# An image tower on one core: the image rows for the second half of each patch are copied inside SBUF in place of a second load from main memory

## The chip, the cores and the metric

The kernel runs on one core of a Trainium2 chip. The core's engines run side by side, each its own program in order: PE (TensorE, matmuls into PSUM), ACT (ScalarE), DVE (VectorE), POOL (GpSimd) and SP (SyncE, which issues most DMAs). They wait for one another through semaphores. Sixteen DMA engines move the data between main memory and the on-chip memory SBUF. The metric is the device time of one execution in microseconds (us).

## What is computed

64 images of 3 x 224 x 224 are cut into patches of 16 x 16 pixels, 14 x 14 = 196 tokens an image. Two transformer layers with mixtures of experts follow:

```python
patches = img.reshape(B, C, Hp, p, Wp, p)
patches = patches.transpose(0, 2, 4, 1, 3, 5).reshape(B, S, C * p * p)
h = jnp.einsum('bsk,ek->bse', patches, w) + b                  # tok, 768 -> 128
h = h + L0_attn(_layernorm(h))     # single head, quantized weights, causal
h = h + L0_ffn(_layernorm(h))      # 8 experts, each takes its 1024 best tokens
h = h + L1_attn(_layernorm(h))     # 8 heads, layernorm on q and k, causal
h = h + L1_ffn(_layernorm(h))      # 8 experts, each token goes to its best 2
```

The change touches the first line of these only: how the pixels get into SBUF.

## The kernel before, in words

The program has four stages. The first, `embed_and_attend`, does patches, first attention and the routing logits of the first expert layer. It takes about the first 430 us. `topk_experts`, `attend_and_route` and `routed_experts` follow; they read what the first has written to main memory.

**Units and iterations.** The first stage works in 32 units of two images (4 tiles of 98 tokens, 392 columns). Its code is written out without a loop, and software-pipelined: iteration n works on the patches of unit n, the first layernorm of unit n-1, the scores of unit n-2, the output of unit n-3 and the second layernorm of unit n-4. ACT and POOL run one unit ahead with `pix`.

**Pixels.** `img` holds raw image rows, 96 partitions x 2 buffers x 2 images x 14 x 224 values. Partition 6r + c holds rows r of every patch of channel c as they are; partition 6r + 3 + c holds the same rows shifted left by 8 pixels. With this one column access at 16 k + j gives pixel j in the lower partitions and pixel j + 8 in the shifted ones, and a patch is embedded in 8 matmuls over 96 partitions. The copy from `img` to `pix` puts the columns j in order: ACT makes j = 0 to 3 (L568, two instructions), POOL j = 4 to 7 (L726, two). Both wait in `image_there` for the DMAs of that buffer (`img_loaded`) and until the unit two back is embedded. PE multiplies (L449, `patch`), ACT adds the bias and writes `hT` (L617).

**Order around the loads.** `load_images` issues twelve DMAs for a unit: for each of 2 images and 3 channels one for the plain rows (L300, 16 partitions x 14 x 224) and one for the shifted rows (L301, 16 x 14 x 216), both from main memory. Unit 0 is loaded in a first block, along with the weights (L305 to L309), while DVE and PE prepare the weights. That block ends for all engines at a barrier. In the second block `emit_sp` runs for n = 1 onwards: wait until the pixels of unit n-2 are copied (`pix_ready`, `pix_ready_pool`), load unit n; for n = 1 issue fourteen small early loads for later stages (L57); store normed tokens and h of unit n-7 (L422, L423), which waits for DVE (`h2_step`); store the logits of unit n-8 (L429), which waits for ACT (`lg_ready`). `img` has two buffers, so SP works about two iterations ahead of PE.

**ACT's order** matters at the start: in `emit_act` the pixels of unit n+1 stand before `hT` of unit n (see `emit` in the listing: `pixels(ahead, ...)`, then L617).

Of the kernel before, what the change touches and what calls it, by code (L numbers as in the profile page):

```python
# [11 lines left out]
IMAGES, CHANNELS, SIDE, PATCH = 64, 3, 224, 16  # L12
GRID = SIDE // PATCH
# [7 lines left out]
UNITS = IMAGES // 2  # L21
# [13 lines left out]
def wait(eng, sem, value, apart=False):  # L35

    if isinstance(value, int) and value <= 0:
        return
    eng.wait_ge(sem, value)
    if apart and not isinstance(value, int):  # L40


        eng.sem_inc(PASSED[str(eng.engine)], 1)  # L43
# [81 lines left out]
def straight(eng, emit, depth, count):  # L125

    for n in range(count + depth):
        emit(n, n)


def live(n, skew, count):
    return not isinstance(n, int) or 0 <= n - skew < count


def build(nc, x, L0_tok_w, L0_tok_b, L0_attn_Wq, L0_attn_Wk, L0_attn_Wv, L0_ffn_Wr, L0_ffn_W1, L0_ffn_b1,
# [3 lines left out]
    with ExitStack() as ctx:  # L139
# [38 lines left out]
        for i, g in enumerate(qk_gains):  # L178
# [3 lines left out]
        early.add(wr_all[:], L0_ffn_Wr)  # L182

        embed_and_attend(nc, sb, ps, sem, early, made, groups, x, L0_tok_w, L0_tok_b, L0_attn_Wq, L0_attn_Wk, L0_attn_Wv, L0_ffn_Wr,
                         hd_dram, ident, ident_b, ones, mask_qk, halfpow, logits_dram, xn_dram)
        chosen = topk_experts(nc, sb, ps, sem, early, wr_all, L0_ffn_W1, b1n_topk, L0_ffn_W2, L0_ffn_b2, hd_dram,
# [35 lines left out]
def span(start, size):  # L222

    return slice(start, start + size) if isinstance(start, int) else bass.ds(start, size)


def embed_and_attend(nc, sb, ps, sem, early, made, groups, x, w_tok, b_tok, wq, wk, wv, wr, hd_dram, ident, ident_b, ones,
                     mask_qk, halfpow, logits_dram, xn_dram):
    with ExitStack() as ph:
        S = lambda name, shape, dt=F32: sb(name, shape, dt, ph)  # L230
        P = lambda name, shape, dt=F32: ps(name, shape, dt, ph)
        half = PATCH // 2
        rows = CHANNELS * PATCH

        img = S("img", [2 * rows, 2, 2, GRID * SIDE])
# [52 lines left out]
        w_copied = sem("w_copied")  # L288
        cstep = sem("const_step")
        n_loads = 6  # L290
        img_loaded = [sem(f"img_loaded{k}") for k in range(2)]
        imgs = x.rearrange("b c (g p) w -> b c p g w", p=PATCH)

        def load_images(sp, u, k):

            for m in range(2):
                dst = img[:, k % 2, m, :].rearrange("r (g w) -> r g w", g=GRID)
                for c in range(CHANNELS):
                    lo, hi = (slice(CHANNELS * s + c, 2 * rows, 2 * CHANNELS) for s in range(2))
                    sp.dma_start(dst[lo], imgs[2 * u + m, c]).then_inc(img_loaded[k % 2], 16)  # L300
                    sp.dma_start(dst[hi, :, 0:SIDE - half], imgs[2 * u + m, c, :, :, half:]  # L301
                                 ).then_inc(img_loaded[k % 2], 16)

        def load_weights(sp):
            sp.dma_start(w_nat[:], w_tok).then_inc(w_loaded, 16)  # L305
            sp.dma_start(bias[:], b_tok.rearrange("(e o) -> e o", o=1)).then_inc(w_loaded, 16)
            for i, w in enumerate((wq, wk, wv)):
                sp.dma_start(w3[:, i, :], w).then_inc(w_loaded, 16)
            sp.dma_start(wr_sb[:], wr).then_inc(w_loaded, 16)  # L309

        with nc.Block() as block:
            @block.sync
            def _(sp):
                load_weights(sp)
                load_images(sp, 0, 0)

            @block.gpsimd
            def _(pool):
# [90 lines left out]
        def emit_sp(sp):  # L409
            def emit(n, k):  # L410

                if live(n, 0, UNITS) and not (isinstance(n, int) and n == 0):
                    wait(sp, pix_ready, 2 * (n - 1), apart=True)
                    wait(sp, pix_ready_pool, 2 * (n - 1))
                    load_images(sp, n, k)
                if isinstance(n, int) and n == 1:
                    early.issue(sp)
                if live(n, 7, UNITS):
                    u = n - 7
                    r = u % 2  # L420
                    wait(sp, h2_step, (u + 1) * H2_STEPS)
                    sp.dma_start(xn_view[:, span(u * TPU, TPU), :], xn2[:, r]).then_inc(xn2_stored[r], 16)  # L422
                    sp.dma_start(hd_view[:, span(u * TPU, TPU), :], h2[:, r]).then_inc(h2_stored[r], 16)  # L423
                if live(n, 8, UNITS):
                    u = n - 8
                    r = u % 2
                    wait(sp, lg_ready, u + 1)
                    for t in range(TPU):
                        sp.dma_start(logits_dram[:, span(u * COLS + t * TILE, TILE)],  # L429
                                     lg[32 * t:32 * t + EXPERTS, r, :]).then_inc(lg_stored[r], 16)  # L430
            straight(sp, emit, 8, UNITS)
            for s in (*xn2_stored, *h2_stored):
                sp.wait_ge(s, 16 * UNITS // 2)
            for s in lg_stored:
                sp.wait_ge(s, 16 * TPU * UNITS // 2)
# [119 lines left out]
            return img[:, k % 2].rearrange("r m (q j) -> r j (m q)", j=PATCH)[:, js, :]  # L555

        def image_there(eng, n, k):
            wait(eng, img_loaded[k % 2], (n // 2 + 1) * 16 * 12 if isinstance(n, int) else
                 (n - (k % 2)) * (16 * 6) + 16 * 12, apart=True)
            wait(eng, embedded, n - 1, apart=True)  # L560

        def emit_act(act):
            def pixels(n, k, first, end):
                if not live(n, 0, UNITS):
                    return
                if first == 0:
                    image_there(act, n, k)
                act.copy(pix[:, k % 2, first:end, :], by_column(k, slice(first, end))).then_inc(pix_ready, 1)  # L568
# [168 lines left out]
        with nc.Block() as block:  # L737
            @block.sync
            def _(sp):
                emit_sp(sp)  # L740

            @block.tensor
            def _(pe):
                emit_pe(pe)

            @block.scalar
            def _(act):
                emit_act(act)

            @block.vector  # L750
            def _(dve):
                emit_dve(dve)

            @block.gpsimd
            def _(pool):
                emit_pool(pool)
# [1750 lines left out]
```

## Time and profile before

| | us |
|---|---|
| median of 3 runs | 1961.18 |
| lowest and highest | 1959.18, 1964.82 |
| profiled execution, first to last instruction (span) | 1907.7 |
| what the median has beyond that span | 53.5 |

| engine | busy, share of the span |
|---|---|
| PE | 1666.0 us, 87% |
| DVE | 1201.1 us, 63% |
| POOL | 1162.9 us, 61% |
| ACT | 1076.6 us, 56% |
| DMA queue q1 (issued by SP) | 206432 packets, 134.16 MB, 28.9% of 16 engines |

The profile is of one execution. Busy shares are averages over four stages with different limits, so the first stage is read by itself, in windows of its time. PE's busy time includes waiting inside its pipeline. A time given with a DMA instruction of SP is how long its issue took; when the data had landed is a number of its own ("to landing"). The image loads are 192 of 196.0 KB and 192 of 189.0 KB, with a median of 4.3 and 4.5 us from issue to landing. The granted clock is a share of TensorE's full 2.4 GHz: 0.50 is the 1.2 GHz level.

### The profile page before, as it was taken

Reading aid. Unit: us, or ns where it says so; the run is one execution under the profiler, and the core shown is the slowest. Engines: PE = TensorE matmul, PEld = TensorE weight load, DVE = VectorE, ACT = ScalarE, POOL = GpSimd, SP = SyncE. Lnnn points to the kernel's source line nnn. Section 1 sums busy time; section 2 is a strip of 40 time slices with the busy share of each in tenths; the row PEclk is TensorE's granted clock in tenths of the full one; section 3 lists DMA queues with packets and bytes.
Section 4 is the critical chain, followed back from the end, with each engine's and each line's share of the span. In section 5 each row is a group of like instructions: output and inputs, shape, how many; then the busy total and the mean of one; then the engine's idle time right before and its main releaser. Section 6 shows DMA issues by size and latency. Waiting matters only on the chain. (4 is left out here: it accounts for less than half of the span.)

```text
span 1907.7 us, 45923 instructions
## 1 busy us (share of the span) xinstructions
PE 1666.0 (87%) x13765; PEld 1251.6 (66%) x13766; DVE 1201.1 (63%) x4836; ACT 1076.6 (56%) x2574; POOL 1162.9 (61%) x1108
## 2 busy tenths in 40 slices
PE   4999999995569764699999999999994999999996
PEld 2666666663447543467667677676662999998995
DVE  2899999983743002678888888888864343433442
ACT  2666666651436432467776776777751555555553
POOL 2455655531057885226776766767656687878876
PEclk8999999995569887699999999999997999999998
DMA  8989999931014433311111111211112455545553
GB/s 198 237 209 222 216 223 234 228 97 52 12 40 78 67 53 60 106 32 48 53 53 51 53 55 46 58 51 53 41 45 62 66 71 65 69 68 65 72 67 40
DMA packets 257801, 172.48 MB, mean 90 GB/s; under 512 B 25598, under 2 KB 250656, under 8 KB 257632
## 3 DMA queue, kind: packets, MB, share of 16 engines
q1 hardware_dynamic: 206432, 134.16, 28.9%
q0 software_dynamic: 50112, 35.64, 13.8%
q8 instruction: 92, 1.51, 0.3%
q10 hardware_dynamic: 1088, 0.53, 0.2%
q14 instruction: 77, 0.63, 0.1%
HBM read 117.64 MB, written 52.40 MB: 89 GB/s over the span
## 5 line engine op out<-in xcount | busy, mean ns | idle before, releaser
L2373 POOL DMA_INDIRECT out_dram<-r_yw,r_idx x212 | 332.5, 1568 | 94.2 <-issue 41.4
L2255 POOL DMA_INDIRECT rows_scratch<-routed_row,slot_u x256 | 254.2, 993 | 169.8 <-DVE slot_u L2194 106.7
L2438 ACT ACTIVATE r_hT<-r_p_up,r_b1T 128x256 f32<-128x256 f32 x424 | 191.6, 474 | 123.4 <-PE r_p_up L2413 120.0
L1920 ACT ACTIVATE a_probsT<-a_p_sc 98x392 f32<-98x392 f32 x384 | 170.7, 501 | 109.7 <-PE a_p_sc L1677 72.0
L2401 PEld LDWEIGHTS r_p_y<-w_all,r_hT 128*128 128x128 f32 x1696 | 224.1, 193 | 11.1
L2413 PE MATMUL r_p_up<-r_xgT,r_w1e 128*128 128x256 f32 x848 | 222.4, 386 | 9.3 <-DVE r_w1e L2453 8.7
L2401 PE MATMUL r_p_y<-w_all,r_hT 128*128 x1696 | 224.8, 276 | 0.0
L449 PE MATMUL p_embed<-pix,w_pix 96*128 96x392 f32 x512 | 209.2, 516 | 3.5 <-ACT pix L568 3.5
L2025 DVE TENSOR_REDUCE a_negmax<-a_p_max 98x2 bf16<-98x392 f32 x256 | 132.5, 559 | 61.4 <-PE a_p_max L1642 61.4
L718 POOL TENSOR_SCALAR vare<-mv 98x4 f32<-98x4 f32 x64 | 29.9, 467 | 218.3 <-DVE mv L703 199.5
L2413 PEld LDWEIGHTS r_p_up<-r_xgT,r_w1e 128*128 128x128 f32 x848 | 147.1, 194 | 22.5 <-issue 8.0
L2459 DVE TENSOR_TENSOR r_yb<-r_p_y,b_all 128x256 f32<-128x256 f32 x106 | 45.0, 425 | 133.5 <-PE r_p_y L2401 130.8
L1666 PE MATMUL a_p_sc<-q_var,kT 32*98 32x196 f32 x1024 | 117.2, 346 | 1.7 <-ACT a_probsT L1920 1.7
L896 POOL DMA_INDIRECT h_scratch<-yw,tok_u x64 | 100.4, 1568 | 28.0 <-issue 18.3
L726 POOL COPY pix<-img 96x784 f32<-96x784 f32 x64 | 95.8, 1526 | 31.6 <-DMA img<-in_x_dram 31.6
L449 PEld LDWEIGHTS p_embed<-pix,w_pix 96*128 96x128 f32 x512 | 89.5, 199 | 38.2 <-issue 6.3
L1703 PE MATMUL a_p_q<-wqkvT,a_xnT 128*98 128x384 f32 x256 | 107.9, 528 | 1.4 <-ACT q_var L1961 0.8
L568 ACT COPY pix<-img 96x784 f32<-96x784 f32 x64 | 98.3, 1542 | 19.1 <-DMA img<-in_x_dram 19.0
L886 POOL DMA_INDIRECT xg<-xn_scratch,tok_u x64 | 62.0, 969 | 75.1 <-DVE tok_u L1183 55.9
L2453 DVE COPY r_w1e<-w_all 128x512 f32 x106 | 48.4, 457 | 85.1 <-issue 60.5
L1201 DVE TENSOR_TENSOR yb<-p_y,b2e 128x512 f32<-128x512 f32 x16 | 11.1, 692 | 142.7 <-PE p_y L1014 142.7
L1014 PEld LDWEIGHTS p_y<-w2e,ffn_hT 128*128 128x128 f32 x512 | 69.8, 201 | 35.8 <-issue 34.4
(377 smaller groups left out, 4171.6 us busy)
## 6 DMA issues: line engine op xcount, KB each, us to landing
img<-in_x_dram SPq DMA_DIRECT2D x192, 196.0 KB, 4.3
img<-in_x_dram SPq DMA_DIRECT2D x192, 189.0 KB, 4.5
r_xg<-rows_scratch SPq DMA_DIRECT2D x106, 130.0 KB
xn_scratch<-xn SPq DMA_DIRECT2D x32, 196.0 KB
h_scratch<-h SPq DMA_DIRECT2D x32, 196.0 KB
h<-h_scratch SPq DMA_DIRECT2D x32, 196.0 KB
h3b<-h_scratch SPq DMA_DIRECT2D x32, 196.0 KB
out_dram<-h SPq DMA_DIRECT2D x32, 196.0 KB
```

What stands on the lines that cost most here:

```text
L449: last = pe.matmul(p_embed[:, 0:COLS], w_pix[:, j, :], pix[:, k % 2, j, :], start=(j == 0), stop=(j == half - 1))
L568: act.copy(pix[:, k % 2, first:end, :], by_column(k, slice(first, end))).then_inc(pix_ready, 1)
L896: pool.indirect_dma_start(hd_dram, bass.IndirectOffsetOnAxis(ap=tok_u[:, u * GT + t:u * GT + t + 1], axis=0), yw[:, u % RINGY, t, :], None ...
L1666: pe.matmul(p_sc[p][:, x * PAIR:(x + 1) * PAIR], kT[rows, s4, o:o + TILE], q_var[rows, s4, var + x, o:o + PAIR], start=(x == 0), stop=Fals ...
L1703: pe.matmul(p_q[t % 2][0:TILE, 0:3 * D], xnT[:, u % 2, t * TILE:(t + 1) * TILE], wqkvT[:], start=True, stop=True).then_inc(qkv, 1)
L1920: act.activation(probsT[:, u % 2, i, :], p_sc[i % 2][:, 0:2 * PAIR], ACT.Exp).then_inc(exped, 1)
L2025: dve.tensor_reduce(negmax[:, u % 2, group + 1, h], src.rearrange("p (h c) -> p h c", h=2), X, ALU.max, negate=True).then_inc(maxed, 1)
L2255: pool.indirect_dma_start(rows_dram, bass.IndirectOffsetOnAxis(ap=slot_u[:, u % ROWS, c, t:t + 1], axis=0), row[:, u % ROWS, c, t, :], Non ...
L2373: pool.indirect_dma_start(acc_dram, bass.IndirectOffsetOnAxis(ap=idx[:, (k - 3) % 4, t:t + 1], axis=0), yw[:, (k - 3) % 4, t, :], None, co ...
L2401: last = pe.matmul(p_y[k % 2][:, t, :], hT[:, (k - 2) % 2, f, t * 128:(t + 1) * 128], w2e[:, bass.ds(e, 1), f, :], start=(f == 0), stop=(f ...
L2413: pe.matmul(p_up[f][:, 0:G], w1e[:, (k - 1) % 2, f * 128:(f + 1) * 128], xgT[:, (k - 1) % 2, :], start=True, stop=True).then_inc(up, 1)
L2438: act.activation(hT[:, (k - 1) % 2, f, :], p_up[f][:, 0:G], ACT.Silu, bias=b1T[:, bass.ds(e * FC + f, 1)]).then_inc(act_h, 1)
```

## The change

The plain rows are loaded as before. The shifted rows are no longer loaded: `shift_images` waits until all six loads of the unit have landed and then issues six DMAs from SBUF to SBUF. Each takes the 16 partitions of one channel and image, from value 8 to the end of the 14 x 224 = 3136, and writes these 3128 values as one run to the partition three further on. (The values that cross a row's end land where no column is read.) The count that ACT and POOL wait for falls from 12 DMAs to 6, now the copies.

```diff
+        img_rows_in = sem("img_rows_in")
...
                 for c in range(CHANNELS):
+                    sp.dma_start(dst[c:2 * rows:2 * CHANNELS], imgs[2 * u + m, c]).then_inc(img_rows_in, 16)
+
+        def shift_images(sp, u, k):
+
+            sp.wait_ge(img_rows_in, (u + 1) * 16 * 2 * CHANNELS)
+            for m in range(2):
+                for c in range(CHANNELS):
                     lo, hi = (slice(CHANNELS * s + c, 2 * rows, 2 * CHANNELS) for s in range(2))
-                    sp.dma_start(dst[lo], imgs[2 * u + m, c]).then_inc(img_loaded[k % 2], 16)
-                    sp.dma_start(dst[hi, :, 0:SIDE - half], imgs[2 * u + m, c, :, :, half:]
+                    sp.dma_start(img[hi, k % 2, m, 0:GRID * SIDE - half], img[lo, k % 2, m, half:GRID * SIDE]
                                  ).then_inc(img_loaded[k % 2], 16)
...
                 load_images(sp, 0, 0)
+                shift_images(sp, 0, 0)
...
                                      lg[32 * t:32 * t + EXPERTS, r, :]).then_inc(lg_stored[r], 16)
+                if live(n, 0, UNITS) and not (isinstance(n, int) and n == 0):
+                    shift_images(sp, n, k)
...
-            wait(eng, img_loaded[k % 2], (n // 2 + 1) * 16 * 12 if isinstance(n, int) else
-                 (n - (k % 2)) * (16 * 6) + 16 * 12, apart=True)
+            wait(eng, img_loaded[k % 2], (n // 2 + 1) * 16 * 2 * CHANNELS, apart=True)
```

Only SP's row of instructions changes; it has 765 before and 507 after. At the start of the second block (L57: early loads, the first and the last shown) before:

```order
L300 DMA img<-in_x_dram 16x14x224
L301 DMA img<-in_x_dram 16x14x216
...
L57 DMA a_w_nat<-in_L_attn_Wq_dram 128x128
...
L57 DMA wr_all<-in_L_ffn_Wr_dram 128x8
L300 DMA img<-in_x_dram 16x14x224 [waits pix_ready_pool,pix_ready]
L301 DMA img<-in_x_dram 16x14x216
```

and after:

```order
L300 DMA img<-in_x_dram 16x14x224 x6
L57 DMA a_w_nat<-in_L_attn_Wq_dram 128x128
...
L57 DMA wr_all<-in_L_ffn_Wr_dram 128x8
L308 DMA img<-img 16x3128 [waits img_rows_in]
L308 DMA img<-img 16x3128 x5
L300 DMA img<-in_x_dram 16x14x224 [waits pix_ready_pool,pix_ready]
L300 DMA img<-in_x_dram 16x14x224 x5
```

The second half of unit 1's rows moved from before the early loads to behind them. In a full iteration on SP, before (twelve image loads, of which three are shown, then the stores):

```order
L300 DMA img<-in_x_dram 16x14x224 [waits pix_ready_pool,pix_ready]
L301 DMA img<-in_x_dram 16x14x216
L300 DMA img<-in_x_dram 16x14x224
...
L422 DMA xn_scratch<-xn 98x4x128 [waits h2_step]
L423 DMA h_scratch<-h 98x4x128
L429 DMA logits_scratch<-lg 8x98 [waits lg_ready]
L429 DMA logits_scratch<-lg 8x98 x3
```

and after:

```order
L300 DMA img<-in_x_dram 16x14x224 [waits pix_ready_pool,pix_ready]
L300 DMA img<-in_x_dram 16x14x224 x5
L430 DMA xn_scratch<-xn 98x4x128 [waits h2_step]
L431 DMA h_scratch<-h 98x4x128
L437 DMA logits_scratch<-lg 8x98 [waits lg_ready]
L437 DMA logits_scratch<-lg 8x98 x3
L308 DMA img<-img 16x3128 [waits img_rows_in]
L308 DMA img<-img 16x3128 x5
```

The stores moved ahead of the second half of the image, and a wait stands between.

## Rows read from the trace of the kernel before

**Rows 1.** The page's slices (40 of 47.7 us): busy tenths of the DMA engines.

```profile
DMA  8989999931014433311111111211112455545553
```

**Rows 2.** Windows: stretch, its length, busy us (instructions) by engine, PEclk, DMA share, GB/s.

```profile
84.80:97.20 12.40, 11.98 (x72) 7.91 (x71) 11.32 (x42) 8.20 (x19) 5.75 (x5) 1.00 1.03 245
...
399.40:411.80 12.40, 11.98 (x72) 7.88 (x71) 11.52 (x44) 8.40 (x20) 6.05 (x7) 1.00 0.13 35
```

**Rows 3.** Timeline, ACT: start, duration, instruction [idle before]; hT of units 18, 29, 30.

```profile
263.52 0.59 ACT L617 ACTIVATE hT<-p_embed,bias 128x392 f32<-128x392 f32 x1 [0.41 <-PE p_embed L449]
...
397.73 0.59 ACT L617 ACTIVATE hT<-p_embed,bias 128x392 f32<-128x392 f32 x1 [0.42 <-PE p_embed L449]
409.93 0.59 ACT L617 ACTIVATE hT<-p_embed,bias 128x392 f32<-128x392 f32 x1 [0.42 <-PE p_embed L449]
```

**Rows 4.** Waits, 0 to 60 us: who waited for whom, us in total, times, longest.

```profile
POOL pix L726 <- DMA img<-in_x_dram: 31.6, 4, 13.3
...
ACT pix L568 <- DMA img<-in_x_dram: 19.0, 2, 11.0
```

**Rows 5.** Timeline, SP: first load of a unit, first store, logits stores.

```profile
234.90 0.59 SPq L300 DMA_DIRECT2D img<-in_x_dram  x1
...
242.68 0.58 SPq L422 DMA_DIRECT2D xn_scratch<-xn  x1
...
243.80 1.92 SPq L429 DMA_DIRECT2D logits_scratch<-lg  x4
```

**Rows 6.** Image loads to landing (16 to 30 us, 100 to 390 us); window 75 to 400 us.

```profile
DMA to landing us min/median/max: 3.3/4.2/5.2
...
DMA to landing us min/median/max: 2.8/4.3/5.8
...
75.00:400.00 325.00, 306.68 (x1812) 203.24 (x1811) 304.17 (x1110) 212.31 (x493) 168.56 (x191) 0.99 0.94 221
```

**Rows 7.** Timeline, ACT: the first copy of the pixels of unit 19.

```profile
256.05 1.53 ACT L568 COPY pix<-img 96x784 f32<-96x784 f32 x1
```

**Rows 8.** DMA issues: transfer, number, KB each, median us to landing.

```profile
lgt<-logits_scratch SPq DMA_DIRECT2D x1, 392.0 KB, 3.0
...
block_rec<-rec SPq DMA_DIRECT2D x8, 24.9 KB, 2.1
```

**Rows 9.** Timeline, SP: first image load, first early load, first load of unit 2.

```profile
3.67 0.76 SPq L300 DMA_DIRECT2D img<-in_x_dram  x1
...
23.07 0.60 SPq L57 DMA_DIRECT2D a_w_nat<-in_L_attn_Wq_dram  x1
...
30.70 0.65 SPq L300 DMA_DIRECT2D img<-in_x_dram  x1
```

**Rows 10.** Timeline, ACT's copies of units 0, 1, 2, 4, and PE on units 1, 2.

```profile
16.60 2.93 ACT L568 COPY pix<-img 96x784 f32<-96x784 f32 x2
...
27.63 2.92 ACT L568 COPY pix<-img 96x784 f32<-96x784 f32 x2 [8.10 <-DMA img<-in_x_dram]
...
31.97 7.68 PE L449 MATMUL p_embed<-pix,w_pix 96*128 96x392 f32 x16
...
43.76 2.92 ACT L568 COPY pix<-img 96x784 f32<-96x784 f32 x2 [10.95 <-DMA img<-in_x_dram]
...
47.22 1.09 PE L455 MATMUL p_htr<-ident,hT 128*98 128x128 f32 x4 [7.56 <-ACT hT L617]
...
63.76 1.54 ACT L568 COPY pix<-img 96x784 f32<-96x784 f32 x1
```

**Rows 11.** A window as in rows 2, and PE's timeline (idle before in brackets).

```profile
122.00:124.00 2.00, 1.75 (x6) 1.40 (x7) 1.78 (x11) 1.65 (x7) 0.07 (x1) 0.50 1.09 264
...
122.25 1.09 PE L455 MATMUL p_htr<-ident,hT 128*98 128x128 f32 x4 [2.24 <-ACT hT L617]
...
123.14 2.82 PE L449 MATMUL p_embed<-pix,w_pix 96*128 96x392 f32 x4
...
239.45 1.48 PE L449 MATMUL p_embed<-pix,w_pix 96*128 96x392 f32 x4
```

## The prediction, made before the changed kernel ran
> **What bounds the kernel now.** I read the page's slices first [rows 1]: the image stage is the first nine or so of 40 (0 to 430 us), and there the DMA engines show 8 or 9 tenths throughout. PE is as full: 11.98 us of 12.40 in a window inside the stage [rows 2]. Two resources look full, and the change takes work from one of them only. So the question is which of the two paces the stage.
>
> Two views answer it. The first is the list of ACT's writes of hT, one for each unit of two images [rows 3]: from unit 18 (263.52 us) to unit 30 (409.93) they stand 146.41 / 12 = 12.20 us apart, without exception. The second is the pair of windows in [rows 2], one with the image traffic at its fullest (DMA share 1.03, 84.8 to 97.2 us), one after the last load (0.13, 399.4 to 411.8). PE is busy 11.98 us in both, ACT 8.20 and 8.40, DVE 11.32 and 11.52, and the hT of unit 30, made without image traffic, still comes 12.20 us after that of unit 29. When the traffic is gone, nothing speeds up. An iteration is paced by the ring of PE, DVE and ACT. **The DMA engines are full but not late.**
>
> The waits agree [rows 4]: all waiting for image data in the first 60 us is 31.6 us of POOL in four waits and 19.0 us of ACT in two, and the same view of 60 to 400 us has no wait for img on any engine.
>
> **The change in a full iteration.** Today SP needs 242.68 - 234.90 = 7.8 us for the twelve loads of a unit, 0.65 each, and 243.80 + 1.92 - 242.68 = 3.0 us for six stores [rows 5]: 10.8 of 12.2 us. After the change: six loads, 3.9 us. The same six stores, 3.0 us, which now come 3.9 us earlier. A wait until the six loads have landed. Then six copies inside the chip. The stores stand between the loads and the wait and cover most of it: the last load is issued 3.25 us into the unit and lands 4.3 us later (median of 100 to 390 us, [rows 6]), at 7.55 us, and the stores end at 6.9. That leaves 0.65 us of waiting.
>
> The issue of a copy isn't in the trace. From below stands a logits store, 1.92 / 4 = 0.48 us, from above an image load, 0.65 us [rows 5]. I take 0.48: the copy (16x3128) is a plain set of rows on both sides like that store, while the load is 16x14x224. Six cost 2.9 us. SP's unit becomes 3.9 + 3.0 + 0.65 + 2.9 = 10.4 us of 12.2, so it still idles for 1.8 us. Queued behind the new wait are the copies and then the next unit's loads and stores. Those loads may start only when the pixels of the unit two back are copied, and that happens once in 12.2 us in any case.
>
> The landing of a copy isn't in the trace either. The nearest rows are block_rec, a transfer within SBUF of 24.9 KB, 2.1 us, and for size lgt, 392 KB in rows of 3 KB, 3.0 us [rows 8]. Above them stands the short-run image load, up to 5.2 us before 30 us [rows 6]. Six copies issued in 2.9 us ask for 1.15 MB / 2.9 us = 400 GB/s, which is more than the 221 GB/s of the loads, so I don't take the low end but 3.0 us. An image is then complete 3.9 + 3.0 + 0.65 + 2.4 + 3.0 = 13 us after SP starts on it. Loads started at 234.90 [rows 5] are for unit 19, whose pixels ACT copies at 256.05 [rows 7], 21 us later. **8 us to spare**, so the steady part pays and gains nothing: 28 x 0. What hides the chain is this double buffer. Without it each unit would pay the difference to today's chain, 7.15 + 4.3 = 11.5 us, so 1.5 us.
>
> Halving the short runs (1344 fewer of 864 bytes in each unit) is worth nothing either, by [rows 2].
>
> One rule of the notes is about the pressure on SBUF; its sentences can be left out. The Trainium skill, "SBUF — State Buffer", section "Door 1: The DMA port swizzle", says that 8 partitions share one of 16 ports of about 27 GB/s and that partitions 0 to 63 reach the 8 even ports only. As an estimate by that page, an even port takes 200 KB of images and 32 KB of stores in a unit, 8.5 us, and with 100 KB that the copies read back 12.2 us, if reads and writes share the port, which the page doesn't say. No row here splits traffic by port. Even so the copies would just fit into an iteration.
>
> **The start, the only place where images are waited for.** Times as in [rows 9, 10]. I lay SP's queue out anew: 0.65 per load, landing 4.3, 0.48 per copy, landing 3.0.
> - Unit 0: the last load is issued at 7.1 and lands at 11.4; copies 11.4 to 14.3, the last issued at 13.8 and there at 16.8. Today SP has issued all by 3.67 + 12 x 0.65 = 11.6 and the barrier opens at 23.07 - 12 x 0.65 = 15.3, so others set it, and SP's 14.3 doesn't move it. ACT starts at 16.8 instead of 16.60. POOL starts at most 1.5 us later than the barrier allows, and PE wants its pixels only after four columns of ACT's.
> - Unit 1: loads 15.3 to 19.2. Then the fourteen early loads, 30.70 - 23.07 = 7.6 us, which now stand ahead of the copies: to 26.8. Copies to 29.7, there at 32.2 against 27.63, **4.5 us later**. PE's matmuls on unit 1, 31.97 to 39.65 before, run 36.5 to 44.2.
> - Unit 2: loads 29.7 to 33.6 (30.70 to 38.5 before), landed 37.2, copies to 40.1, there at 42.6 against 43.76. ACT makes hT of unit 1 only after its copies for unit 2. Before, PE was done at 39.65 and sat idle for 7.56 us, until ACT had its image at 43.76. Now PE is done at 44.2 and ACT at 42.6 + 2.9 = 45.5. hT comes 1.2 us earlier than before. **The 4.5 us are taken out of an idle time that was there anyway: -1.2.**
> - Unit 3: loads 40.1 to 44.0, landed 47.7, copies 50.5, there at 53.1: 10.5 us after unit 2, less than an iteration.
> - Unit 4: loads from 50.5, landed 58.1, copies there at 63.5; wanted at 63.76 - 1.2 = 62.6. Left: -0.3.
> - Unit 5 is there 10.4 us later, and wanted about 12 later. From here SP gains in every unit.
>
> **Sum.** Span 1907.7 + 0 (steady) - 0.3 (start) = 1907.4 us, and 1961.18 - 1907.7 = 53.5 us lie around it (the page gives the span alone, so this is the median less the span): 1960.9, that is **1961 us**, the median of the runs shown. What follows the stage is the same work on the same data.
>
> **Rivals.**
> *A. SP's serial chain becomes the bound (slower).* Load, land, copy must fit into 12.2 us, and that is where it decides. With 0.65 us a copy and 5.2 us of landing the chain is 3.25 + 5.2 + 3.9 = 12.35 us. With 5 us for a copy's landing, the start then gives: unit 1 at +7.3, unit 2 at 47.3 (+3.5), unit 4 at 72.0 (+8.2), unit 5 +9, and 0.15 more for each later unit. 1970, at worst 1974 us. For it: the longest landing of the stage is 5.8 us [rows 6]. Against: that is with twelve loads a unit, and the median is 4.3.
>
> *B. The copies are slow (slower).* In a unit 2.31 MB of images and 0.40 MB of stores move at 221 GB/s at a DMA share of 0.94 [rows 6], so 235 GB/s when busy. The remaining 1.58 MB take 6.7 us, which leaves 5.5 us for 1.15 MB of copies. It decides below 210 GB/s. At 120 GB/s a unit takes 16.3 us: 28 x 4.1 = +115, 2076 us. For it: each copy is one run of 12.5 KB on each engine, from one partition to one, and no row shows this form. Against: lgt moves 392 KB in 3.0 us, of which 2.1 are there for small transfers too [rows 8].
>
> *C. The start gets quicker (faster).* With copies landing in 2.1 us and loads in 3.3, unit 2 is there at 40.7, and hT of unit 1 comes when PE is done, near 43.8, 2.8 us earlier. PE's idle time ahead of unit 2 shrinks from 7.56 us to about 1. After an idle time of 2.24 us at 120 us the granted clock was 0.50, the 1.2 GHz level, and the next four matmuls of p_embed took 2.82 us [rows 11]; at 2.4 GHz four take 1.48. If the clock stays up, another 2 or 3 us. Together 1956 us.
>
> **Chances.** About 0.3% (6 us) is what a measurement of this kernel can tell from no change. My forecast, with the small outcomes of A and C that stay inside it: 0.76. A beyond it: 0.11; B: 0.06; both are slower, 0.17. C beyond it, which needs a little more than its 1956: 0.07. The range takes in A's 1970 and C's 1956 with the scatter of the runs shown (1959.18 to 1964.82) around them: 1954 to 1972. B is left out.
>
> **What would show it.** Right: hT every 12.20 us from unit 18 on; SP waiting for image rows some 0.65 us in a unit; a copy issued in 0.48 us and there in about 3; ACT's wait for unit 1 near 12.6 us instead of 8.10 and for unit 2 near 5.5 instead of 10.95; a DMA share of the stage under 0.94. Wrong: a wait for img on ACT or POOL after 80 us, or hT further apart than 12.20 in the regular part. With idle DMA engines that is A, with full ones B.

## The result: 0.5% slower, all of it lost in the first 110 us

| | before | after |
|---|---|---|
| median of 10 runs each, us | 1957.03 | 1968.37 |
| lowest and highest, us | 1952.11, 1964.82 | 1961.39, 1970.86 |
| ratio after / before, 95% interval | | 1.0047 [1.0029, 1.0064] |
| data read from main memory, MB | 117.64 | 80.48 |

The kernel got slower by 0.47%, some 9 us. (The ratio goes by all the runs; the two medians alone stand 11.3 us apart.) The main memory now delivers 37 MB less, and nothing is gained from it. The forecast was no change.

The levels differ between chips: the same kernel before took 1908.67 and 1906.66 us on two of them, 1953.39 and 1954.93 us on two others, so only ratios taken on one chip, and times inside the first stage, are compared below.

The steady part is as fast as before. The views of [rows 3] and [rows 2], now of the changed kernel: ACT's hT of units 18, 29 and 30, and the two wide windows of the first stage with the one between 300 and 390 us.

```profile
274.44 0.59 ACT L626 ACTIVATE hT<-p_embed,bias 128x392 f32<-128x392 f32 x1 [0.40 <-PE p_embed L459]
...
408.65 0.59 ACT L626 ACTIVATE hT<-p_embed,bias 128x392 f32<-128x392 f32 x1 [0.41 <-PE p_embed L459]
420.85 0.59 ACT L626 ACTIVATE hT<-p_embed,bias 128x392 f32<-128x392 f32 x1 [0.41 <-PE p_embed L459]
```

```profile
0.00:75.00 75.00, 40.97 (x121) 23.54 (x122) 23.43 (x100) 21.31 (x30) 20.19 (x28) 0.86 0.71 184
75.00:400.00 325.00, 305.54 (x1787) 201.53 (x1787) 299.87 (x1097) 210.52 (x491) 167.69 (x191) 0.99 0.85 224
...
300.00:390.00 90.00, 87.03 (x513) 57.09 (x512) 84.67 (x321) 59.91 (x140) 45.50 (x47) 1.00 0.87 226
```

Again (420.85 - 274.44) / 12 = 12.20 us a unit. The DMA share from 75 to 400 us fell from 0.94 [rows 6] to 0.85. But the whole row of hT stands about 11 us later: unit 18 at 274.44 instead of 263.52, unit 30 at 420.85 instead of 409.93. Where the delay arises, the same list of hT shows (us; the second row of before is another execution of that kernel, experiment e1):

| hT of unit | 0 | 1 | 2 | 3 | 6 | 31 |
|---|---|---|---|---|---|---|
| before, the profile ahead | 30.46 | 46.58 | 58.77 | 70.39 | 107.56 | 422.32 |
| before, again | 30.39 | 46.44 | 59.65 | 71.27 | 108.06 | 421.43 |
| after | 38.45 | 50.78 | 63.89 | 80.11 | 118.02 | 433.25 |

At unit 6 the delay is 10 us, and it stays. (Units 8 and 16 vary from execution to execution. From hT of unit 7 to that of unit 8 the profile ahead took 14.93 us, with a granted clock of 0.50 from 122 to 128 us, and e7 below 12.43, with the clock at 1.00. So the last times agree only to some 2 us for one kernel, and to 3 or 4 between kernels; unit 6 is the better mark.)

The waits, as in [rows 4] for 0 to 60 us, then the rows of the same view for 60 to 400 us, where before had none:

```profile
POOL pix L735 <- DMA img<-img: 34.1, 3, 16.4
...
ACT pix L577 <- DMA img<-img: 22.3, 3, 13.8
...
POOL pix L735 <- DMA img<-img: 9.6, 4, 4.1
ACT pix L577 <- DMA img<-img: 6.8, 6, 3.0
```

SP's timeline of the start (start, duration of all x instructions together; L308 is the copies, L300 the loads; the fourteen early loads are left out but for the first):

```profile
3.67 4.00 SPq L300 DMA_DIRECT2D img<-in_x_dram  x6
11.53 4.05 SPq L308 DMA_DIRECT2D img<-img  x6
16.22 3.89 SPq L300 DMA_DIRECT2D img<-in_x_dram  x6
20.16 0.60 SPq L57 DMA_DIRECT2D a_w_nat<-in_L_attn_Wq_dram  x1
...
27.72 4.12 SPq L308 DMA_DIRECT2D img<-img  x6
31.95 3.91 SPq L300 DMA_DIRECT2D img<-in_x_dram  x6
40.05 4.06 SPq L308 DMA_DIRECT2D img<-img  x6
44.21 3.92 SPq L300 DMA_DIRECT2D img<-in_x_dram  x6
52.95 4.04 SPq L308 DMA_DIRECT2D img<-img  x6
57.53 3.92 SPq L300 DMA_DIRECT2D img<-in_x_dram  x6
65.11 4.81 SPq L308 DMA_DIRECT2D img<-img  x6
70.03 4.01 SPq L300 DMA_DIRECT2D img<-in_x_dram  x6
78.19 4.03 SPq L308 DMA_DIRECT2D img<-img  x6
...
90.64 4.03 SPq L308 DMA_DIRECT2D img<-img  x6
```

From 52.95 to 90.64 us three units pass, 12.56 us each: six copies 4.05, six loads 3.9, and between the end of the loads and the first copy 4.2 on average (48.13 to 52.95, 61.45 to 65.11, 74.04 to 78.19). There are no stores yet to cover that wait. ACT's copies of the pixels of units 0, 1, 2 and 4, to hold against [rows 10]:

```profile
18.88 2.94 ACT L577 COPY pix<-img 96x784 f32<-96x784 f32 x2 [1.37 <-DMA img<-img]
35.63 2.92 ACT L577 COPY pix<-img 96x784 f32<-96x784 f32 x2 [13.81 <-DMA img<-img]
47.96 2.92 ACT L577 COPY pix<-img 96x784 f32<-96x784 f32 x2 [7.16 <-DMA img<-img]
...
73.54 1.51 ACT L577 COPY pix<-img 96x784 f32<-96x784 f32 x1 [2.95 <-DMA img<-img]
```

These are 2.3, 8.0, 4.2 and 9.8 us later than before. Between units 2 and 4 the kernel before lets 63.76 - 43.76 = 20.0 us pass [rows 10], since the pipeline is still filling and its iterations are short; the changed one needs 73.54 - 47.96 = 25.6. **That is the point where a chain of 12.56 us is too long, though the steady iteration of 12.20 nearly bears it.** ACT writes hT of unit 3 behind these pixels of unit 4, and that hT is 80.11 - 70.39 = 9.7 us late, as late as the pixels. PE's clock adds nothing to it in this execution. It was low for a while before the images came (windows as in [rows 2]), and 1.00 from 68 us on:

```profile
64.00:66.00 2.00, 1.48 (x5) 1.20 (x6) 0.00 (x0) 1.54 (x6) 0.00 (x0) 0.62 0.11 25
66.00:68.00 2.00, 2.00 (x5) 0.93 (x4) 1.66 (x9) 0.23 (x1) 0.36 (x1) 0.53 0.32 100
```

ACT was through with its own work at 70.6 us and then still waited 2.95 us for the images.

A steady unit of SP, to hold against [rows 5]:

```profile
390.90 4.04 SPq L308 DMA_DIRECT2D img<-img  x6
395.04 3.98 SPq L300 DMA_DIRECT2D img<-in_x_dram  x6
399.06 0.58 SPq L430 DMA_DIRECT2D xn_scratch<-xn  x1
399.69 0.45 SPq L431 DMA_DIRECT2D h_scratch<-h  x1
400.18 2.22 SPq L437 DMA_DIRECT2D logits_scratch<-lg  x4
403.21 3.94 SPq L308 DMA_DIRECT2D img<-img  x6
```

That is 12.31 us, and (403.21 - 341.05) / 5 gives 12.43 over the last five units. SP has hardly any idle time left. It falls behind the engines by about 0.2 us a unit, and keeps up only because the slower units around 8 and 16 had given it room: its copies start 27.4 us ahead of the hT of their unit at unit 6, 34.2 at unit 18 (240.28 and 274.44 us), and 30.0 again at unit 30 (390.90 and 420.85).

### The profile page after: what moved, and what is told of

Read it like the earlier page. It is cut to its first block, busy times and chain, and to the rows that moved or that the text cites. A ratio compares the mean times of both kernels' runs of the same rounds, so it can differ in the third digit from the quotient of the medians.

```text
span 1969.1 us, 45923 instructions
## 1 busy us (share of the span) xinstructions
PE 1698.4 (86%) x13765; PEld 1262.4 (64%) x13766; DVE 1198.3 (61%) x4836; ACT 1076.2 (55%) x2574; POOL 1162.2 (59%) x1108
## 3 DMA queue, kind: packets, MB, share of 16 engines
HBM read 80.48 MB, written 52.40 MB: 67 GB/s over the span
## 4 chain that ended last, share of the span: by engine, by line
PE 23%; POOL 16%; DVE 13%; issue 11%; DMA 9%; ACT 2%; POOLq 1%; DVEq 0%; SPq 0%; another core or an unknown queue 0%; ACTq 0%
DMA out_dram<-r_yw,r_idx 7%; POOL h_scratch L905 4%; POOL out_dram L2382 4%; POOL rows_scratch L2264 3%; PE a_p_q L1712 3%; POOL qkn L2272 3%; PE a_p_av L1751 3%; PE a_p_sc L1675 3%; DVE a_negmax L2034 2%; PE r_p_up L2422 2%; POOL xg L895 2%; DVE var_h L2153 2%; PE r_p_y L2410 2%; PE a_p_sc L1689 2%; PE a_p_q L1604 2%
## 5 line engine op out<-in xcount | busy, mean ns | idle before, releaser
L1675 PE MATMUL a_p_sc<-q_var,kT 32*98 32x196 f32 x1024 | 125.1, 353 | 6.0 <-ACT a_probsT L1929 2.2
L1023 PEld LDWEIGHTS p_y<-w2e,ffn_hT 128*128 128x128 f32 x512 | 75.8, 217 | 71.6 <-issue 67.5
L1023 PE MATMUL p_y<-w2e,ffn_hT 128*128 128x128 f32 x512 | 78.1, 303 | 35.4 <-DVE yb L1210 24.1
## 6 DMA issues: line engine op xcount, KB each, us to landing
img<-img SPq DMA_DIRECT2D x192, 195.5 KB, 3.0
```

The lines of the kernel that those rows point to most:

```text
L1023: last = pe.matmul(p_y[:, t, :], hT[:, n % 2, f, t * 128:(t + 1) * 128], w2e[:, (n // PG) % 2, f, :], start=(f == 0), stop=(f == FC - 1))
L1675: pe.matmul(p_sc[p][:, x * PAIR:(x + 1) * PAIR], kT[rows, s4, o:o + TILE], q_var[rows, s4, var + x, o:o + PAIR], start=(x == 0), stop=Fals ...
```

## Experiments

**The kernel before once more (e1)**, to have the two kernels' first stages from one chip.

> The kernel before, unchanged, profiled once more. The prediction took 53.5 us to lie outside the span of 1907.7 us. If that is so, this profile has a span near 1908 again. If instead the profiled execution was a quick one (the changed kernel's runs have spans only 1.8 us below their times), the span is near 1955, the image stage is as before (last hT near 422.3 us), and the extra 45 to 50 us stand in later stages.

Measured: 1952.63 us, span 1950.9, hT as in the table. Against the profile ahead (span 1907.7) the first stage ends within 1 us at the same place (421.43 and 422.32). The 43 us that the spans differ by lie behind it, most of them in the second attention: its score matmuls run from 808.1 to 1477.5 us here, and from 796.2 to 1433.6 in the profile ahead. Why is open.

**Short copies (e2).** From unit 2 on each copy moves 391 of its 3128 values, so the rest of the shifted rows is stale.

```diff
+                    run = (GRID * SIDE - half) // (8 if u >= 2 else 1)
-                    sp.dma_start(img[hi, k % 2, m, 0:GRID * SIDE - half], img[lo, k % 2, m, half:GRID * SIDE]
+                    sp.dma_start(img[hi, k % 2, m, 0:run], img[lo, k % 2, m, half:half + run]
```

> The changed kernel, but from unit 2 on each of the six copies moves 391 values per partition in place of 3128 (this leaves out seven eighths of the shifted rows). The number of issues, waits and their order stay. Theory A (SP's own chain of issue, wait, issue paces the start and costs the 10.9 us): SP still spends about 4.0 us on six copies, its units stay 12.3 to 12.7 us apart in the start, last hT at 430 to 433 us (433.3 in the changed kernel, 422.3 before). Theory D (the copies' data keep the DMA engines and the landings long): last hT falls to 425 or less, and the copies' issue gets shorter with their size.

**No copies (e9).** From unit 2 on they are left out, and ACT and POOL wait for the six loads; the shifted rows of those units are stale.

```diff
-            for m in range(2):
+            for m in range(2 if u < 2 else 0):
...
-            wait(eng, img_loaded[k % 2], (n // 2 + 1) * 16 * 2 * CHANNELS, apart=True)
+            if n < 2:
+                wait(eng, img_loaded[k % 2], (n // 2 + 1) * 16 * 2 * CHANNELS, apart=True)
+            else:
+                wait(eng, img_rows_in, (n + 1) * 16 * 2 * CHANNELS, apart=True)
```

> The changed kernel without any copy from unit 2 on (this leaves out the shifted rows of 30 units); ACT and POOL wait for the loaded rows, and SP still waits for them where the copies stood. Against e2_short_copies (425.8, short copies) it tells what the issuing and landing of six tiny copies costs apart from their bytes. If SP's issue of the copies is what is left of the loss, last hT is at 421 to 423. If it stays at 425 to 426, what is left comes from units 0 and 1, whose copies are still made.

Measured, hT (us) beside after:

| hT of unit | 0 | 1 | 2 | 3 | 6 | 31 |
|---|---|---|---|---|---|---|
| before, again | 30.39 | 46.44 | 59.65 | 71.27 | 108.06 | 421.43 |
| after | 38.45 | 50.78 | 63.89 | 80.11 | 118.02 | 433.25 |
| e2, an eighth of the data | 38.47 | 48.26 | 60.03 | 75.82 | 112.39 | 425.77 |
| e9, no copies from unit 2 | 38.27 | 48.11 | 59.68 | 75.60 | 112.18 | 428.79 |

The last hT of e9 lies past both values that had been expected of it; its units 8 and 16 alone took 15.17 and 15.62 us (e2: 13.60 and 13.97), so unit 6 is compared. Two things follow. The issue of six copies, still 3.72 us in e2, costs nothing by itself: e2 and e9 differ by 0.2 us. With the full copies unit 6 comes 118.02 - 112.39 = 5.6 us later. The bytes do this by way of SP's chain, which neither theory of e2 had. SP's timeline of e2 at units 2 and 4:

```profile
40.04 3.72 SPq L309 DMA_DIRECT2D img<-img  x6
...
63.26 3.73 SPq L309 DMA_DIRECT2D img<-img  x6
```

A unit takes 11.6 us there in place of 12.56, since the loads of the next land sooner, and ACT has its data 1.8 us after the last copy was issued (unit 2) instead of 4.8. And even without any copy behind unit 1 the start loses 112.18 - 108.06 = 4.1 us. The late first two units are made good at unit 2 (59.68 against 59.65, as the prediction said), and then 4.3 us are lost again in unit 3: 15.92 us from hT to hT, where before took 11.62.

The windows of 300 to 390 us (length, busy us by engine, PEclk, DMA share, GB/s) of the kernel before, of e2 and of e9 also price the copies as traffic.

```profile
300.00:390.00 90.00, 87.03 (x511) 57.09 (x511) 84.67 (x322) 59.93 (x142) 45.12 (x47) 1.00 0.96 230
```

```profile
300.00:390.00 90.00, 86.68 (x520) 57.17 (x520) 84.93 (x323) 59.97 (x143) 41.90 (x42) 1.00 0.61 147
```

```profile
300.00:390.00 90.00, 87.04 (x523) 58.25 (x522) 84.80 (x314) 61.22 (x139) 44.45 (x44) 1.00 0.52 127
```

Here "before" is execution e1. From e9 to after the rate rises by 226 - 127 = 99 GB/s and the share by 0.87 - 0.52 = 0.35, so copies move at 99 / 0.35 = 283 GB/s of busy time. Rival B needed less than 210. PE is busy 87 us of 90 in all four.

**The wait covered (e7).** All copies are made, but each image's three are issued as soon as that image's three loads are in. (The loads count up img_rows_of[m], and one small semaphore of the setup is merged into another.)

```diff
-            sp.wait_ge(img_rows_in, (u + 1) * 16 * 2 * CHANNELS)
             for m in range(2):
+                sp.wait_ge(img_rows_of[m], (u + 1) * 16 * CHANNELS)
                 for c in range(CHANNELS):
...
```

> The changed kernel with a semaphore for each of the two images of a unit: SP waits for the three rows of image 0, issues their copies, and then waits for image 1, whose landing the first copies cover. Same DMAs, same data, same order of issue. Theory A (waiting and issuing on SP paces the start): the unit at the start shrinks from 12.6 to about 10.7 us, unit 2 comes 2 us earlier, units 3 and 4 four, the rows wait nearly goes in steady state, last hT near 428 (433.3), total 4 to 5 us below the changed kernel. Theory D (the data of the copies, queued ahead of the next loads, set the pace): the data are the same, last hT within 1.5 us of 433.3.

Measured: ratio 0.9999 [0.9983, 1.0015], hT of unit 6 at 112.49 us. SP's wait for rows, in the waits of the whole span (total, times, longest), first in the changed kernel, then in e7:

```profile
SPq L308 <- DMA img<-in_x_dram: 44.0, 29, 4.8
```

```profile
SPq L307 <- DMA img<-in_x_dram: 15.0, 12, 2.2
```

SP's copies of units 2 and 4 in e7:

```profile
37.14 4.07 SPq L307 DMA_DIRECT2D img<-img  x6
...
58.19 5.27 SPq L307 DMA_DIRECT2D img<-img  x6
```

That is 10.5 us a unit (10.7 had been expected), and unit 6 comes where it came without any copy (112.18). **The same number of copies with the same bytes no longer costs these 5.6 us once the second image's loads land under the first image's copies.** So they were the chain load, land, copy on SP, not the copies' traffic as such. The ratio of the whole change falls from 1.0047 to 0.9999, level with the kernel before as far as the interval tells (3 us to either side); the first stage still ends 2 to 3 us late (hT of unit 31 at 424.71).

**The clock (e10).** Now the 4.1 us that the start loses without the copies. In e9 PE sits idle for 2.99 us, waiting for the hT of unit 2, and then runs slowly. Windows and PE's timeline of e9:

```profile
60.00:62.00 2.00, 1.69 (x6) 1.35 (x7) 0.00 (x0) 1.55 (x6) 0.00 (x0) 0.50 1.02 239
...
64.00:66.00 2.00, 2.00 (x8) 1.32 (x7) 1.38 (x3) 0.49 (x1) 1.92 (x3) 0.50 0.00 1
```

```profile
60.31 1.09 PE L465 MATMUL p_htr<-ident,hT 128*98 128x128 f32 x4 [2.99 <-ACT hT L629]
```

The granted clock is 0.50, the 1.2 GHz level, from 60 to 68 us. e10 is e9 with 14 more matmuls at unit 3, ahead of PE's wait, so that PE is not idle there.

```diff
-                    wait(pe, hT_ready, u + 1)
                     wait(pe, h_ready, u)
+                    if n == 3:
+                        for _ in range(14):
+                            pe.matmul(p_htr[:, 0, :], ident[:, 0:TILE], ident[:], start=True, stop=True)
+                    wait(pe, hT_ready, u + 1)
```

> The kernel without copies from unit 2 on (the upper row groups of those units hold stale rows), and with 14 more matmuls of the identity into p_htr at unit 3, ahead of PE's wait for hT; they leave no other result changed. Theory clock: in the run without copies hT(2) came at 59.68 us, level with the kernel before (59.65), and hT(3) at 75.60 in place of 71.27, since PE had waited 2.99 us up to 60.3 and its granted clock was 0.50 from 60 to 68 us. With PE at work in that wait the clock in 60 to 68 us should be 1.00 in place of 0.50, hT(3) come near 71.5 and hT(6) near 108 us in place of 112.2. Theory images: the 4 us of unit 3 are a wait for image rows or an engine behind them; then hT(3) stays near 75.6 and the clock has no part in it.

Measured, the same windows and the same transposes in e10:

```profile
60.00:62.00 2.00, 2.00 (x13) 1.39 (x12) 0.89 (x5) 1.04 (x4) 0.00 (x0) 1.00 1.03 220
...
64.00:66.00 2.00, 2.00 (x18) 1.83 (x17) 1.56 (x2) 2.00 (x4) 2.00 (x3) 1.00 0.00 0
```

```profile
59.78 0.64 PE L465 MATMUL p_htr<-ident,hT 128*98 128x128 f32 x4
```

hT of unit 3 at 70.76 instead of 75.60, of unit 6 at 107.63 instead of 112.18, level with the kernel before (107.56 and 108.06). The theory of the clock holds: more work on PE took 4.6 us away. (0.5 us of them were there before the added matmuls ran: hT of unit 2 came at 59.14 instead of 59.68. From hT of unit 2 to that of unit 3 it is 11.62 us instead of 15.92, so 4.3.) Each of e9 and e10 is a single execution. The kernel before pays for one such stretch as well, but cheaply. The low clock begins in its long idle time ([rows 10], 7.56 us up to 47.22):

```profile
44.00:46.00 2.00, 0.00 (x0) 0.00 (x0) 0.00 (x0) 2.00 (x2) 2.00 (x2) 0.50 1.13 221
...
48.00:50.00 2.00, 2.00 (x5) 1.10 (x4) 1.00 (x6) 0.59 (x1) 0.00 (x0) 0.50 1.14 233
```

Part of it passes while PE has nothing to do, and from hT of unit 1 to that of unit 2 takes 12.2 to 13.2 us, against 11.6 in e9. So e9 does not have one more stretch than the kernel before; it has it at unit 3, where it costs 4.3 us, and not where it costs 0.6 to 1.6.

**Both cures together (e13):** e7 with the 14 matmuls.

> The changed kernel with all its copies, each image's copies issued as soon as that image's rows are in, and 14 more matmuls of the identity into p_htr at unit 3, in PE's wait of 2.65 us for hT. Theory clock: what the per-image order left over the kernel before (hT(3) 75.92 against 71.27 us, hT(6) 112.49 against 107.56) is the low clock at 68 to 75 us; with PE at work in the wait the granted clock in 68 to 74 us is 1.00, hT(3) comes near 71 us, hT(6) near 108, the last hT 420 to 422, and the ratio is 0.997 to 0.999. Theory copies: the copies' own landings hold unit 3 back; then hT(3) stays over 74 us and the ratio near 1.000. Should the stretch of low clock only move to another unit (PE also waits 1.98 us at 66.3 us there), hT(3) stays near 76 us with the clock at 0.50, and neither theory is told apart.

Measured: granted clock 1.00 from 58 to 78 us, hT of unit 3 at 73.43 (e7: 75.92), of unit 6 at 110.27 (e7: 112.49), ratio 1.0007 [0.9996, 1.0017]. Half of what was expected, and no time that the runs can tell from e7's. In this execution the clock was 0.50 from 50 to 56 us, where e7 had 1.00, so PE reached the added matmuls only at 59.44 us and had no wait left to fill with them. It was in them until 62.5, while hT of unit 2 had been there since 60.23, 2.2 us earlier. Those 2.2 us are about the missing half. That the copies themselves hold nothing back is not contradicted, but not shown by the median either.

**The changed kernel again (e11).**

> The changed kernel as it is, timed and profiled once more beside the others. Theory chain (SP's serial unit of copies, loads and landings binds in the start, and the clock is paid once): hT(6) near 118 us, last hT at 431 to 434 us, ratio to the kernel before 1.003 to 1.0065. Theory chance (the 0.47% came from the one placing of clock stretches in one series of executions): ratio within 1.002 and last hT near 425 us.

Measured: ratio 1.0046 [1.0028, 1.0063], hT of unit 6 at 118.70, of unit 31 at 431.84. The result repeats, stage times included.

**Copies from unit 2 on (e12).** Units 0 and 1 are loaded twice, as before.

```diff
+                    if u < 2:
+                        lo, hi = (slice(CHANNELS * s + c, 2 * rows, 2 * CHANNELS) for s in range(2))
+                        sp.dma_start(dst[lo], imgs[2 * u + m, c]).then_inc(img_loaded[k % 2], 16)
+                        sp.dma_start(dst[hi, :, 0:SIDE - half], imgs[2 * u + m, c, :, :, half:]
+                                     ).then_inc(img_loaded[k % 2], 16)
+                        continue
...
```

> Units 0 and 1 are loaded twice, as in the kernel before; copies begin with unit 2. This takes away the late hT(0) (38.45 us in place of 30.39) and leaves the copies of all later units. Theory chain: hT(0) and hT(1) come as before, near 30.4 and 46.5 us, then SP's unit of 12.5 to 12.7 us loses time against the 12.2 us of the engines; hT(6) at 112 to 115 us and last hT at 427 to 430 us, ratio 1.002 to 1.004. Theory start (the late first image is the whole loss): hT(6) near 108, last hT near 421.5 us, and ratio within 1.001.

Measured: ratio 1.0032 [1.0017, 1.0047]; hT of units 0, 1, 2, 3 and 6 at 30.39, 48.87, 61.48, 78.96 and 116.33. The late first image is not the whole loss: with it cured, 8.3 of 10 us at unit 6 remain. Unit 6 is 1.3 us past what I had allowed. SP issues copies at 38.15, 50.46 and 62.66 us, 12.3 apart (then 75.62 and 88.06), and ACT has its pixels of unit 4 at 70.86 instead of 63.76: seven of the eight us are the chain during the fill. So the 4.1 us of e9 and the 5.6 us between e2 and the changed kernel are not two losses side by side in the latter. Its images alone make unit 3 as late as it is, the 4.1 us show only where the chain is cured, and curing the first image alone gives back some 2 us. In e12 the late images make PE wait in its stead; from 74 to 78 us the granted clock there is 0.58.

**The early loads.** They stand ahead of the copies of unit 1 and hold them back until 27.72 us. e4 moves them in the changed kernel to n = 10. e5 moves them in the kernel before, and e8 in e7, behind the last image:

```diff
-                if isinstance(n, int) and n == 1:
+                if isinstance(n, int) and n == UNITS:
                     early.issue(sp)
```

> The changed kernel with the fourteen early loads issued at unit 10 in place of unit 1, so the copies of unit 1 don't stand behind them. Theory A: copies of unit 1 start when its loads have landed, near 24 instead of 27.7 us, so everything of the start comes 3.7 us earlier, and the rest of the loss (SP's unit of 12.5 us) stays: last hT near 429.5, total near 1964.5. If the place of the early loads is all of it, last hT comes near 423 and the total near 1958.

> The kernel before, with nothing but the fourteen early loads moved from unit 1 to behind the last image load. SP then starts on unit 2 at 23.2 instead of 30.8 us and that image is there near 36 instead of 43.8. PE's idle time ahead of hT of unit 1 goes: hT of unit 1 near 40.5 (46.4), last hT near 416 (421.4), total 4 to 6 us below the kernel before. If the start of the kernel before is held up by something else (DMA engines, full from 33 us on), it gains less than 2 us.

> As e7_per_image, and the fourteen early loads moved behind the last image. Theory A: everything of the start another 3.7 us earlier, and no fourteen issues in SP's full iterations: last hT near 423, total within 3 us of the kernel before. It should not beat e5_before_early_last, whose start has no chain of two transfers.

| | ratio to before | hT of unit 1 | 6 | 31 |
|---|---|---|---|---|
| e4 | 1.0045 [1.0031, 1.0060] | 46.73 | 114.61 | 434.98 |
| e5 | 0.9959 [0.9946, 0.9973] | 40.64 | 101.88 | 418.19 |
| e8 | 0.9970 [0.9960, 0.9979] | 41.12 | 103.09 | 416.30 |

e4 wins 3.4 us by unit 6 and loses it later: at n = 10 the same 7.5 us of issues fall on an SP that has next to no time left, and from unit 22 to 29 hT stands 12.3 to 14.0 us apart. That is neither of its two theories (429.5 or 423), but it fits a steady chain as full as the rows say. Where SP has slack (e5) or gets it (e8), moving them behind the images gains 4 to 6 us at unit 6 against the kernel before, and 3 to 6 at unit 31. The total of e5 fell by 7.8 us, more than the 4 to 6 expected and more than its first stage gained (3 to 4); where the rest arose was not looked into. **e5 beats both kernels**, and does so without the change; e8, with the change, has an interval that overlaps e5's.

**Half as many copies (e3)**, a failed cure: three copies of 16 x 2 x 3128, both images in one.

```diff
-            for m in range(2):
-                for c in range(CHANNELS):
-                    sp.dma_start(img[hi, k % 2, m, 0:GRID * SIDE - half], img[lo, k % 2, m, half:GRID * SIDE]
+            for c in range(CHANNELS):
+                sp.dma_start(img[hi, k % 2, :, 0:GRID * SIDE - half], img[lo, k % 2, :, half:GRID * SIDE]
...
-            wait(eng, img_loaded[k % 2], (n // 2 + 1) * 16 * 2 * CHANNELS, apart=True)
+            wait(eng, img_loaded[k % 2], (n // 2 + 1) * 16 * CHANNELS, apart=True)
```

> The changed kernel with both images of a unit in one copy per channel: three copies of 16 x 2 x 3128 in place of six of 16 x 3128, the same bytes. Theory A: SP's unit is 2.0 us shorter (three issues of 0.67), images of unit 1 come 2 us earlier, of unit 2 four, and the start stops losing: last hT near 426, SP waits for pixels again in steady state, total 6 to 8 us below the changed kernel, near 1961. Theory D: same data, so last hT stays at 432 to 434 and the total at 1968.

Measured: ratio 1.0154 [1.0131, 1.0177], some 30 us slower where 6 to 8 us less than the changed kernel had been expected. From unit 3 on hT stands 12.8 to 14.2 us apart until the last image is in, and ACT waits for images 31 times. SP's timeline of one unit, and the landings:

```profile
213.86 2.47 SPq L307 DMA_DIRECT2D img<-img  x3
216.43 5.68 SPq L300 DMA_DIRECT2D img<-in_x_dram  x6
...
227.06 2.47 SPq L307 DMA_DIRECT2D img<-img  x3
```

```profile
img<-in_x_dram SPq DMA_DIRECT2D x192, 196.0 KB, 4.8
img<-img SPq DMA_DIRECT2D x96, 391.0 KB, 4.7
```

The copies' issue fell from 4.05 to 2.47 us, but that of the six loads behind them rose from 3.9 to 5.68, so the sum, 8.15 us, is what it was (7.95). The landings grew by 0.7 and 1.7 us, and the chain with them to 13.2 us a unit (213.86 to 227.06). Here the chain is the bound of the whole stage, and it is what rival A described. Why the loads' issue takes longer here is open; that they wait for room in the DMA queue would fit, but no run here shows it, and the kernel before, which has no copies, also has loads of 0.8 to 0.9 us around 53 and 74 us.

## Why the prediction was wrong, by its steps

The step that failed is the length of SP's unit: 10.4 us were added up, and 12.56 (start) and 12.43 (steady) came out, so that SP lost in every unit of the fill in which it had been forecast to gain. The issue of the copies and the last landings of a batch were sized too low. What the prediction had named as the sign of rival A came: ACT waited for an image at 85.88 us (0.71 us), with a DMA share of 0.74 from 75 to 110 us (before: 1.02).

- **"Paced by the ring of PE, DVE and ACT; the DMA engines are full but not late": right.** The share fell from 0.96 to 0.52 in e9, and hT stayed 12.20 us apart.
- **"I take 0.48" for a copy's issue: wrong.** Six took 4.05 us, 0.67 each. I had chosen the lower of two bounds because the form looked like a store's; the load's 0.65 was the better neighbour. +1.15 us a unit.
- **"Landing 3.0 for the last copy": wrong.** 3.0 is the median of single copies. The last of six was issued near 31.2 us at unit 1 and ACT had its data at 35.63, so 4.4. For the loads I used 4.3 from the last issue, which leaves 3.65 of waiting in the start; the rows show 3.7 to 4.8. (In steady state the forecast wait of 0.65 us a unit was about right: 17.6 us in the 23 units from 100 to 390 us, 0.77 each.) Medians of single transfers were put in where the last of a batch counts.
- **"SP's unit becomes 10.4 us of 12.2": this step decided it.** It took 12.43 us in steady state and 12.56 in the start. The 8 us of slack did not hold: all but 0.4 us of the waits for images after 60 us fall before 110. Later there was some, but less. The last copy for unit 19 was issued at 255.8 us, landed within 4.3, and ACT took it at 266.97, 6 us later, and by unit 30 SP's lead had shrunk by another 4.
- **"From here SP gains in every unit": wrong, and the costly error.** With 10.45 us a unit in the start SP would have gained. With 12.56 it lost, since the fill wants two units in 20.0 us. Unit 4 came at 73.54 us (I said 63.5).
- **"The 4.5 us are taken out of an idle time that was there anyway": right in its mechanism**, shown by e9 (hT of unit 2 level with before). But unit 1 came 8.0 us later, not 4.5. The 3.5 us are 1.2 of copy issue, 1.4 of the last landing, and 0.9 of a gate I had put behind another: unit 0's copies ended at 15.6 us, and the barrier opened at 16.2 instead of 15.3. In the changed kernel itself hT of unit 2 is not level but 4.2 us late, by the images.
- **The clock was priced on the wrong side.** Rival C counted it as a possible gain. I never asked where the stretch of low clock falls once the idle times move. With the copies from unit 2 on left out it moved into full work, and cost 4.3 us in unit 3 (e9, e10). What it costs in the changed kernel is not shown: in its profile hT of unit 3 is no later than its images. In e11 the clock was 0.50 from 74 to 80 us and that hT came 2.0 us later still, but at unit 6 0.7 were left.
- **Rival A was the mechanism**, with its price: 0.65 us a copy, the start at +8.2 at unit 4 (measured 9.8), in all 9 us slower (measured 9 by the ratio; that 1970 and 1968.37 are so near is in part chance, since the kernel before now has 1957.03 and not 1961.18). Its loss of 0.15 us in each later unit did not show in hT. I gave it 0.11, because the longest landing was of twelve loads a unit. Its condition was sharper than I saw: in the start it decides below 12.2.
- **Rival B: refuted** by 283 GB/s. The DMA share of 300 to 390 us is 0.87 at an unchanged 12.20 us. That speaks neither for nor against the rule of the Trainium skill ("SBUF — State Buffer", section "Door 1: The DMA port swizzle"): the estimate of 12.2 us by it would have fitted too.
- **"53.5 us lie around the span": wrong, without effect on the difference.** The profiled execution of after took 1970.86 us and has a span of 1969.1, so 1.8 lie around it. The span of before (1907.7) fits an execution at the level of the quicker chips (1908.67), the median that of the others.

## What to carry to other kernels

When loads are replaced by load, wait, copy on one queue, add up that queue's whole unit with the dearest neighbour's issue cost and the last landing of a batch, and hold it against the shortest interval of the pipeline's fill, not only against the steady one. Overlap the wait (issue each part's copies when that part has landed) before judging the idea. Moving images by some microseconds also moves the stretches of low clock on PE: ask of each of its idle times what work follows, and whether something else is waited for there anyway.

## What the runs showed of the hardware

- A copy within SBUF of 195.5 KB, from 16 partitions to 16 others in runs of 12.5 KB, is issued in 0.67 us and lands in 3.0 us (median of 192; the last of six 4.4 and 4.8 at units 1 and 2), and such copies move 283 GB/s of busy DMA time beside the image loads.
- Behind three copies of 391 KB six loads took 0.95 us each to issue, behind six of 195.5 KB 0.65 (e3, after).
- An idle time of 2.99 us on PE was followed by about 8 us at a granted clock of 0.50, which cost 4.3 us; 14 matmuls without use in that place removed it (e9, e10). The length of the idle time alone doesn't tell: in e7 one of 2.65 us, up to 59.5 us, was followed by a clock of 1.00, and one of 1.98 us, up to 68.3, by 0.50 until 74.
- One program stood at two levels on four chips, 1908.67 and 1906.66 us against 1953.39 and 1954.93, with the first stage equal within 1 us in the two profiles that there are. Each chip ran one series only.
